# Four instead of two Toeplitz blocks as three split products, and the convolution's residual added to the gathered tile

## What is computed

```python
x = x + einsum('bct,bcd->bdt', x, W0[cond])            # layer 0, a 64x64 matrix for each batch
x = x + lora_mlp(x)                                    # layer 1, hidden size 2752, LoRA by batch
x = x + s4_conv(x)                                     # layer 2
x = x + einsum('bct,bcd->bdt', x, W3[subj]) + bias     # layer 3
```

```python
K = 2.0 * einsum('hn,hnl->hl', Ct, exp(P)).real        # 64 channels x 1024 taps
y = irfft(rfft(u, n=2*L) * rfft(K, n=2*L)[None])[..., :L] + u * D[:, None]
return y * mask[:, None, :]                            # mask: l < length[b]
```

## Time and profile before

| | |
|---|---|
| profiled execution | 1816.11 us, its span 1814.5 us |
| median of 3 runs | 1816.24 us (1814.32 to 1817.92) |
| PE busy | 1715.8 us, 95% of the span |
| PEld busy | 1470.7 us, 81% |
| DVE busy | 1129.6 us, 62% |
| ACT busy | 687.0 us, 38% |
| POOL busy | 175.2 us, 10% |
| convolution stage, first PE matmul to first transpose | 1625.20 to 1773.01 us |
| layer 3 | 1773.01 us to the end |

### The profile page before, as it was taken

The page is one execution under the profiler, slowest core; times in us unless marked ns, Lnnn a source line. Parts: engine busy times, 40 slices in busy tenths (PEclk is TensorE's granted clock), DMA queues, the critical chain, the costliest instruction groups (busy, mean ns, idle before and its releaser), DMA issues.

```text
span 1814.5 us, 29058 instructions
## 1 busy us (share of the span) xinstructions
PE 1715.8 (95%) x8904; PEld 1470.7 (81%) x8904; DVE 1129.6 (62%) x1695; ACT 687.0 (38%) x1095; POOL 175.2 (10%) x282
## 2 busy tenths in 40 slices
PE   5679999999998999998999999999989899999998
PEld 5568888888888888886888888888877778879997
DVE  2566676676665554334666766766657843448887
ACT  3233333333333443232333333333323422236655
POOL 3442000000000000000000000000010004402330
PEclk9789999999999999999999999999989999999999
DMA  5787233233325564554333333332325534467754
GB/s 196 216 272 212 94 112 102 92 107 103 99 87 197 174 214 162 206 175 147 111 102 99 103 105 98 107 104 90 101 80 182 177 133 140 162 240 238 240 178 186
DMA packets 106660, 269.52 MB, mean 149 GB/s; under 512 B 17142, under 2 KB 22038, under 8 KB 105590
## 3 DMA queue, kind: packets, MB, share of 16 engines
q1 hardware_dynamic: 81334, 210.54, 35.6%
q0 software_dynamic: 12544, 36.29, 6.2%
q10 hardware_dynamic: 12736, 22.16, 3.2%
HBM read 225.12 MB, written 61.64 MB: 158 GB/s over the span
## 4 chain that ended last, share of the span: by engine, by line
PE 44%; DVE 5%; issue 1%; SPq 1%; ACT 1%; DMA 0%; ACTq 0%; DVEq 0%
PE ps L1070 30%; PE ps L1320 5%; PE ps L1317 3%; PE ps L1108 2%; PE ps L1349 1%; DVE whl L1721 1%; PE ps L1333 1%; SPq L435 1%; PE ps L1145 1%; PE ps L1147 1%; DVE act_hl L1725 0%; DVE x1s L1735 0%; SPq L432 0%; DMA wraw<-in_wd 0%; ACT whl L744 0%
## 5 line engine op out<-in xcount | busy, mean ns | idle before, releaser
L1070 PE MATMUL ps<-act_hl,whl 128*128 128x512 f32 x2016 | 466.0, 393 | 10.6 <-DVE act_hl L1725 7.1
L1070 PE MATMUL ps<-xop,aop_a 128*128 128x512 f32 x2016 | 474.4, 391 | 0.0
L1070 PEld LDWEIGHTS ps<-act_hl,whl 128*128 128x128 f32 x2016 | 379.8, 189 | 95.1 <-DVE act_hl L1725 11.5
L1070 PEld LDWEIGHTS ps<-xop,aop_a 128*128 128x128 f32 x2016 | 374.1, 189 | 74.5
L1070 PE MATMUL ps<-xop,aop_b 128*128 128x512 f32 x1512 | 367.7, 392 | 6.8 <-DVE t L1687 6.7
L1070 PEld LDWEIGHTS ps<-xop,aop_b 128*128 128x128 f32 x1512 | 280.1, 189 | 61.9 <-DVE t L1687 6.9
L1721 DVE TENSOR_TENSOR whl<-wraw,whl 128x1024 fp32r<-128x1024 f32 x96 | 118.9, 1238 | 244.7 <-ACT whl L744 244.2
L744 ACT ACTIVATE whl<-wraw 128x1024 fp32r<-128x1024 f32 (+2 forms) x132 | 114.9, 887 | 357.9 <-PE ps L1070 289.1
L1658 DVE TENSOR_TENSOR aop_b<-raw,aop_b 128x512 fp32r<-128x512 f32 x84 | 58.0, 691 | 107.7 <-ACT aop_b L744 107.6
L744 ACT ACTIVATE aop_a<-asum 128x512 fp32r<-128x512 f32 x84 | 48.7, 625 | 163.9 <-DVE asum L1650 160.2
L1108 PEld LDWEIGHTS ps<-t_hl,lb_hl 128*128 128x128 f32 x672 | 97.2, 190 | 9.9
(11 more groups left out here) (222 smaller groups left out, 2020.3 us busy)
## 6 DMA issues: line engine op xcount, KB each, us to landing
wraw<-in_wd SPq DMA_DIRECT2D x88, 512.0 KB, 3.4
raw<-in_wgu SPq DMA_DIRECT2D x168, 256.0 KB, 3.1
rtoep<-k_dram SPq DMA_DIRECT2D x64, 512.0 KB, 4.6
lb_raw<-bgu_of_batches SPq DMA_DIRECT2D x84, 256.0 KB, 3.9
act_raw<-act_dram SPq DMA_DIRECT2D x84, 256.0 KB, 3.4
act_dram<-t ACTq DMA_DIRECT2D x42, 256.0 KB, 2.0
act_dram<-u ACTq DMA_DIRECT2D x42, 256.0 KB, 2.0
xn<-in_x SPq DMA_DIRECT2D x16, 512.0 KB, 6.5
```

What stands on the lines that cost most here:

```text
L1070: ins = pe.matmul(bank, wt, r, start=start and k == 0 and n == 0, stop=stop and k == nk - 1 and n == 2, skip_group_check=True)
```

## The change

`SPLIT` becomes 4, so `TS` becomes 512: blocks d = 2 (192 columns) and d = 3 (160 columns) are done as three fp32r products each instead of one fp32 matmul each. ACT's first copy becomes 128x512 and its second 128x512; DVE's `toep_l` becomes 128x512. The tiles `toep_h` and `toep_l` double, and `w3hi`, `w3lo` move to another address, where they lie behind `ostage`.

The residual addition takes `ug[:, j]` as its first input instead of the strided `x1h`; its output stays the strided `x1h`. Since `ug[:, j]` is now read until the addition is over, POOL's copy of channel h waits for `x2_done` of channel h - 4 in place of `conv_done` of channel h - 4. The first four copies stand ahead of the loop and have no such wait.

```diff
-SPLIT = 2
+SPLIT = 4
 TS = SPLIT * P
...
-        assert at <= xr_base + KB * TOK * 4
-        (w3hi, w3lo), at = place(xr_base + KB * TOK * 4, [
-            ("w3hi", [P, PAIRS, P], F32R), ("w3lo", [P, PAIRS, P], F32R)])
         assert at <= top
-        (yv, x2hi, x2lo, ostage), _ = place(top, [
+        (yv, x2hi, x2lo, ostage, w3hi, w3lo), _ = place(top, [
             ("yv", [P, 2, KB, B], F32), ("x2hi", [P, 2, T], F32R), ("x2lo", [P, 2, T], F32R),
-            ("ostage", [P, 2, T], F32)])
+            ("ostage", [P, 2, T], F32), ("w3hi", [P, PAIRS, P], F32R), ("w3lo", [P, PAIRS, P], F32R)])
...
+            def channel_out(h, j):
+                pool.tensor_copy(ug[:, j, :, :].rearrange("p l (c b) -> p l c b", c=NCH),
+                                 x1h[:, :, :, :, h]).then_inc(ug_ready, 1)
+
+            for j in range(URING):
+                channel_out(j, j)
+            with pool.Fori(1, C // URING) as g:
                 for j in range(URING):
-                    pool.wait_ge(conv_done, g * URING + (j + 1 - URING + CREDIT_CONV))
-                    pool.tensor_copy(ug[:, j, :, :].rearrange("p l (c b) -> p l c b", c=NCH),
-                                     x1h[:, :, :, :, g * URING + j]).then_inc(ug_ready, 1)
+                    pool.wait_ge(x2_done, g * URING + (j + 1 - URING + CREDIT_Y))
+                    channel_out(g * URING + j, j)
...
                 dve.wait_ge(y_done, h + (1 + CREDIT_Y))
-                xh = x1h[:, :, :, :, h]
-                tt(xh, xh, y.rearrange("p l (c b) -> p l c b", c=NCH), ALU.add).then_inc(x2_done, 1)
+
+                tt(x1h[:, :, :, :, h], ug[:, j, :, :].rearrange("p l (c b) -> p l c b", c=NCH),
+                   y.rearrange("p l (c b) -> p l c b", c=NCH), ALU.add).then_inc(x2_done, 1)
```

More of the change, by code:

```diff
@@ L728, in _ @@
             x1h = x1s[:, :, :, :].rearrange("p c l (b h) -> p l c b h", h=C)
-            with pool.Fori(0, C // URING) as g:
+            def channel_out(h, j):
[4 more added lines that the diff above has]
+            with pool.Fori(1, C // URING) as g:
                 for j in range(URING):
-                    pool.wait_ge(conv_done, g * URING + (j + 1 - URING + CREDIT_CONV))
-                    pool.tensor_copy(ug[:, j, :, :].rearrange("p l (c b) -> p l c b", c=NCH),
-                                     x1h[:, :, :, :, g * URING + j]).then_inc(ug_ready, 1)
+                    pool.wait_ge(x2_done, g * URING + (j + 1 - URING + CREDIT_Y))
+                    channel_out(g * URING + j, j)
             pool.wait_ge(w3_hi, 1)
```

## The result

The changed kernel takes 1833.38 us, the median of 4 runs (1832.21 to 1834.74), against 1816.70 (4 runs) for the kernel before: a ratio of 1.0089, 95% interval 1.0071 to 1.0106. It is slower by 16.7 us; the forecast was 1838.0 us, +21.9, with a range of 1816.5 to 1842. The profiled execution took 1833.77 us, its span is 1831.7.

A forecast was written before the change was run, and what follows sets the result against it. PE bounds the kernel before at 2.18 us a channel; after the change DVE would, at 2.56. 59 steps x 0.38 = 22.4, + 0.5 start - 2.0 end + 1.0 layer 3 = +21.9: 1838.0 us, range 1816.5 to 1842.

The forecast's parts named there:

- the lock: In the convolution loop, POOL's copy and DVE's two-SBUF-input subtractions exclude each other; the moved copy adds 0.48 us to DVE's chain.
- u_lo lasts 0.86: DVE's u_lo subtraction in the loop, waiting behind POOL's copy, should last about 0.86 us instead of 0.41.
- The copy's record: POOL's copy in the loop should last about 1.1 to 1.2 us instead of 0.65, waiting for toep_l.
- PE's term: Six fp32r products replace two fp32 blocks on PE in the loop: from 2.18 to 2.25 us a channel.
- Rival (c): On PE, fp32r products of 192 or 160 columns are paid by columns: PE 2.12, total 1810.2 us; chance 0.04.
- The addition: DVE's residual addition in the loop: the strided write alone still needs 0.72 us, despite the contiguous read.
- My chain of 2.56: DVE's loop chain: 0.56 + 0.72 + (0.32 + 0.28) + 0.48 + 0.29 - 0.09 = 2.56 us a channel, above PE's 2.25.
- rival (b): In the loop the addition takes 0.56 us, DVE 2.40 a channel: +11.6, total 1827.7 us; chance 0.12.
- The start: Stage start: longer toep_l among the four copies about +0.3 us, PE's first two channels at half clock +0.2.
- The end: Last channels up to the first transpose: w3lo stops channel 61's addition instead of u_lo of channel 63; -2.0 us.
- Layer 3's start at half clock: After the stage's end PE has been idle, so layer 3 begins at the lower clock: +1.0 us (0 to 1.7).
- A sign that did not show: In the loop PE should have idle time released by DVE, about 0.3 us a channel.

The follow-up runs named there:

- e3: The changed kernel with one further wait, so POOL's copy of channel h also waits for conv_done of channel h - 3 and runs beside yv: 1824.05 us, ratio 1.0037.
- e1: Against the kernel before, only the four split blocks; the addition reads the strided state and the copy waits for conv_done as before: 1825.77 us, ratio 1.0052.
- e9: Changed kernel with two split blocks, addition writing contiguous yv, reading strided state in odd channels and ug in even; output incomplete: 1816.27 us, one execution.
- e6: The changed kernel with only the addition's input put back to the strided x1h instead of ug: 1842.82 us, ratio 1.0137.
- e8: The changed kernel run once more with nothing altered: median 1834.5 us, ratio 1.0092.
- e2: The changed kernel with SPLIT = 2, so only the residual part (addition reads ug, late copy) differs from the kernel before: 1817.27 us, ratio 0.9998.
- e4: The changed kernel with two split blocks and the copy of channel h also waiting for conv_done of channel h - 3: 1816.55 us, ratio 0.9991.
- e10: The kernel before with only w3lo moved after the last addition, in four pieces, layer 3 waiting for the first: 1814.73 us, ratio 0.9986.
- e5: e4 with w3lo formed only after the last addition, in four pieces, layer 3 waiting for the first: 1814.26 us, ratio 0.9981.
- e7: The changed kernel with three split blocks instead of four (SPLIT = 3): 1822.7 us, ratio 1.0029.

## Why the prediction was right, and where it was off

**That DVE becomes the bound through the lock: right, and shown.** e3 takes the copy out of DVE's way by one wait and changes nothing else, and the loop falls from 2.405 to PE's 2.253. The copy's 0.50 and u_lo's 0.28 are close to the 0.48 and 0.29 read from the earlier trace rows. u_lo lasts 0.86, as forecast. The copy's record lasts 0.85 and not the forecast 1.1 to 1.2: it is issued 0.33 us after toep_l's start, later than the forecast had it, so less of the wait for toep_l falls into the record. The loop does not feel this, as the copy still waits until toep_l ends.

**PE's term: right.** 2.253 a channel in e1 and e3 against my 2.25. Three products of 192 or 160 columns cost what three of 224 do. Rival (c), products paid by their columns, is out.

**The addition: the step that failed.** I took "taking one away leaves the other", 0.72 with 0.63 to the next start. The record does last 0.64, but toep_l starts 0.47 after it, since read and write side each have a price and the prices add (e9; e6 shows the read's share again in the loop's time). My chain of 2.56 was too long by that 0.16: 59 x 0.16 = 9 us of forecast that did not come. In the loop that is the middle case, rival (b), whose 2.40 is the slope measured; I had given it 0.12. Its total of 1827.7 us is nonetheless 5.7 below the measured time, for it has the same start as the forecast. The Trainium skill (Advanced Engine Details and Errata, section SBUF Cachelines) has a penalty for each access that goes to another line, and makes no difference between reading and writing. The runs agree that both sides pay, but not the same: 0.19 us for the read and 0.13 for the write.

**The start: a second error, the other way.** I had +0.5 for start and cold clock, and 1.1 for the first steps of the loop; the profile shows +5.3, with PE at half clock for 16.2 us from its first matmul instead of 6.0. e8 shows 7.7 and +1.7, close to what I had. So of the 16.4 us by which the first profile's stage is longer, some 3.6 did not come again in e8. The two errors partly cancel in that profile, -9 and +4: that 1838.0 lies within 5 us of the measured 1833.4 is in part luck. In e8 the code ahead of the stage and layer 3 took 1.9 us more than in the first profile, so its whole time is only 2.0 us less.

**The end: right in kind.** The first transpose comes 8.9 us after yv(60) instead of 11.8, -2.9 against -2.0, and w3lo stands beside the addition of channel 61, as forecast:

```profile
1782.08 4.53 POOL L739 TENSOR_TENSOR w3lo<-wbd,w3hi 128x2048 fp32r<-128x2048 f32 x1 [2.34 <-ACT w3hi L1045]
1782.25 4.80 DVE L1896 TENSOR_TENSOR x1s<-ug,yv 128x256 f32<-128x256 f32 x1
...
1788.86 0.64 PE L1336 MATMUL ps<-ident,x1s 128*128 128x128 f32 x2 [3.69 <-DVE x1s L1896]
```

Layer 3's start at half clock cost 1.3, against 1.0.

**A sign that did not show.** I expected PE to be idle for 0.3 us a channel. PE's busy share is 123.74 of 124 us: matmul records of 0.28 us that start 0.11 apart cover a gap of 2.405 - 2.253 = 0.15, half of what I expected, as DVE's chain was shorter. The bound had to be read from the chain and from the weight loads (120.75 of 124).

**What stays open.** Counted from its first matmul of the stage, PE was busy at half clock for 3.4 to 7.7 us in every execution but one, the first profile of the changed kernel with 16.2. e8 is the same kernel with 7.7, e1 with the four blocks has 7.6, and e6, with the four blocks and the late copy, 6.3. Each is one execution. Why the first profile stands apart is not settled, nor how often such an execution comes.

Nor is it fully settled why the code ahead of the stage, the same in all kernels, ends up to 6 us later in some executions. The traces show where a part of it arises: the profiles of e1, e2, e3, e4, e6 and e8 have a stretch at half clock near 1497 us that the others lack (granted clock 0.50 from 1497.7 to 1500.5 in e3, 1.00 in the kernel before), and PE's 500 matmuls around it take 96.1 to 96.6 us there against 94.5 to 94.8. This limits what the medians can tell to 2 or 3 us, and so terms are compared within the stage. The stage's terms are of one profile for each kernel: the 3.1 us that e2 gains there, and the 3.0 of e4, do not show clear of noise in their medians.

## What to carry to other kernels

When a wait of a POOL copy is moved, ask what DVE does at the new moment: beside yv, which has one SBUF input, the copy cost DVE nothing, or 0.08 us where it ran on into the addition; between two subtractions of SBUF tiles it cost its full 0.5 us, and one more wait, which delays it to the next harmless moment, took that back. Ask also whether DVE has the room: at 2.12 us of 2.18 the same copy was free. Price a replaced matmul by the distance of its weight loads: as no product of 32 to 224 columns here took less than 0.112 us, two fp32 records of 160 columns (0.27 us) are cheaper than three fp32r products (0.34). And look for one long POOL instruction near the end of a stage: 4.7 us of w3lo held the lock while the last channels waited, and putting it after them won 0.14% (e10) to 0.19% (e5).

## What the runs showed of the hardware

- A DVE addition over 256 float32 elements a partition, 256 bytes apart: 0.34 us to the next start with both sides contiguous, 0.47 with a strided write, 0.53 with a strided read (e9), 0.64 to 0.67 with both. The next instruction starts 0.08 before the record's end with a contiguous write, 0.17 before it with the strided write alone, so the duration alone misleads by up to 0.1.
- Where a POOL copy and a DVE subtraction with two SBUF inputs both waited for the running DVE instruction, the copy went first when issued 0.06 us or more ahead (e2, e7, e9, changed), DVE when they were issued within 0.02 us of each other (e2). In e6 two of some 57 channels went the other way: u_lo went first, at 1710.74 and 1725.82 us, though the copy had been issued 0.34 earlier.
- PE was busy from 1626.0 to 1642.2 us in the changed kernel's first profile and stayed at 1.2 GHz all that time.
